# First sweep of a graph network: source rows gathered once per tile of edges into a ring, and copied from it slot by slot

## What is computed

```python
h = relu(layernorm(x))
# layer 0, GATv2, 4 heads of 64
m     = leaky_relu((h @ W_l + b_l)[src] + (h @ W_r + b_r)[dst] + edge_attr @ W_e)
alpha = einsum('ehf,hf->eh', m, att)          # a score per edge and head
a     = softmax of alpha over the edges of each dst (self loops too)
x     = x + relu(batchnorm(mean over heads of segment_sum((h @ W_l)[src] * a, dst) + bias))
# layer 1
h = relu(layernorm(x))
x = x + segment_mean(h[src], dst) @ w_l.T + h @ w_r.T + b
```

## Time and profile before

| what | us |
|---|---|
| median of 3 runs (5717.72 to 5723.28) | 5718.3 |
| the profiled execution | 5719.17 |
| its span, first to last instruction | 5717.8 |
| preparation, to the first transpose of the first sweep | 148.2 |
| first sweep, to VectorE's last copy | 148.2 to 2246.5 |
| maxima over segments | to about 2335 |
| second sweep | to about 3400 |
| third sweep | 3740 to 5660 |

### The profile page before, as it was taken

One profiled execution on the slowest core, in us unless ns is written; L12 is line 12 of the kernel. 1 busy time (PEld: TensorE's weight loads), 2 busy tenths in 40 slices (PEclk: granted clock), 3 DMA queues, 4 the chain that ended last, 5 costly groups with the idle time before them and its releaser, 6 DMA issues. The chain is left out here.

```text
span 5717.8 us, 78439 instructions
## 1 busy us (share of the span) xinstructions
PE 4023.6 (70%) x16956; PEld 2971.5 (52%) x16957; DVE 3389.3 (59%) x8725; ACT 1205.2 (21%) x4481; POOL 3734.5 (65%) x3702
## 2 busy tenths in 40 slices
PE   4888888888888886699999998454444444434445
PEld 3666666666666665344444456343333333333335
DVE  7666666666666666899999999732322322223223
ACT  2111111111111112566666645200000000000000
POOL 4677777777777775366556640167777777777774
PEclk9999999999999999799999998555555555555555
DMA  9444444444444443343434431211111111111112
GB/s 145 117 130 131 133 129 130 132 129 132 130 131 129 132 131 90 96 112 112 112 108 111 112 85 30 60 23 27 27 27 27 27 27 27 27 27 27 27 27 38
DMA packets 638020, 481.93 MB, mean 84 GB/s; under 512 B 453175, under 2 KB 464849, under 8 KB 637573
## 3 DMA queue, kind: packets, MB, share of 16 engines
q1 hardware_dynamic: 465852, 252.92, 17.5%
q0 software_dynamic: 104800, 108.55, 10.8%
q10 hardware_dynamic: 67177, 118.49, 5.7%
HBM read 351.85 MB, written 126.92 MB: 84 GB/s over the span
## 5 line engine op out<-in xcount | busy, mean ns | idle before, releaser
L586 POOL DMA_INDIRECT ZR<-hD,mS x1664 | 1589.0, 955 | 582.4 <-issue 492.6
L1361 POOL DMA_INDIRECT BIG<-h2D,mS x1564 | 1475.7, 944 | 706.7 <-issue 471.5
L1385 PE MATMUL PS<-BIG,ZR 128*128 x3328 | 805.1, 427 | 1128.3 <-SPq L1338 952.5
L1385 PEld LDWEIGHTS PS<-BIG,ZR 128*128 128x128 f32 x3328 | 737.3, 328 | 1196.1 <-SPq L1338 1016.7
L1404 DVE TENSOR_TENSOR BIG<-BIG,PS 128x64 f32 x1664 | 362.3, 218 | 1356.0 <-PE PS L1385 1319.7
L616 PE MATMUL PS<-Wz,R 128*128 128x264 f32 x3328 | 1062.6, 402 | 81.2 <-issue 80.3
L644 DVE SCALAR_TENSOR_TENSOR PS<-PS,a 128x528 f32<-128x528 f32 x832 | 596.0, 716 | 798.9 <-PE PS L617 792.1
L898 PE MATMUL PS<-R,ZR 128*128 128x329 f32 x3328 | 1025.9, 468 | 24.7 <-POOL R L884 16.9
L617 PE MATMUL PS<-BIG,R 128*128 x3328 | 1033.9, 393 | 0.0
L884 POOL TENSOR_TENSOR R<-ZR,R 128x768 f32<-128x768 f32 x416 | 615.8, 1480 | 414.2 <-ACT R L870 412.3
L912 DVE TENSOR_TENSOR BIG<-BIG,PS 128x329 f32 x1664 | 813.2, 489 | 13.4 <-PE PS L898 7.7
(11 more groups left out here) (258 smaller groups left out, 2319.6 us busy)
## 6 DMA issues: line engine op xcount, KB each, us to landing
zD<-ZR ACTq DMA_DIRECT2D x416, 256.0 KB, 2.2
ZR<-zD SPq DMA_DIRECT2D x416, 256.0 KB, 2.6
R<-relD SPq DMA_DIRECT2D x105, 512.0 KB
ZR<-ea SPq DMA_DIRECT2D x1664, 32.0 KB
ZR<-hD,mS POOLq DMA_INDIRECT x1664, 2.5
BIG<-h2D,mS POOLq DMA_INDIRECT x1564, 2.4
AL<-hD SPq DMA_DIRECT2D x28, 224.0 KB, 2.8
lmS<-lmD SPq DMA_DIRECT2D x106, 32.0 KB, 1.8
```

The lines of the kernel that those rows point to most:

```text
L586: Q.indirect_dma_start(zring[:, j % 32, 0, :], None, hD, bass.IndirectOffsetOnAxis(mS[:, j // 16, j % 16:j % 16 + 1], 0)).then_inc(hs[q], 16)
L1361: Q.indirect_dma_start(BIG[:, j * F:j * F + F], None, h2D, bass.IndirectOffsetOnAxis(mS[:, (j // 16) % 4, j % 16:j % 16 + 1], 0)).then_inc ...
L1385: ins = P.matmul(bank3(j // 4)[:, j % 4, :], oh[:, (j // 4) % 4, j % 4, :], rows, start=True, stop=True)
```

## The change

1. `gather_sources` makes one gather per tile (1564, written out without a loop), not per slot. Its target is a ring `HT` of 128 tiles, which lies over the end of `BIG` and the start of `R`. GpSimd itself waits for landings, two quads of gathers late, and counts them in `landed`. It may be 6 quads (24 tiles) ahead of the copies plus what the copies released (`hf`).
2. ScalarE's `keep_turned` copies each slot's rows (128 x 64) from the ring into `zring`, one quad ahead of TensorE. The ring's offset comes from registers (16 loaded from DRAM table `ringD` every 16 slots), and the number of landings to wait for from another 16 (table `needD`, every 64 slots). Its loop is now 64 slots long, not 32. TensorE waits for `hc` from ScalarE in place of the gathers' semaphores.
3. The source numbers come by one plain DMA (`dSr`) at the start. They are turned before the layer norm, and kept in SBUF: 256 columns in `lmS`, the others through `srcD` into the end of `AL`. The 13 indirect DMAs of source rows, `metaS` and SyncE's loads of it go away. `needD` is written twice.
4. `FLG` is loaded after the sweep, since the ring lies on its place: in two pieces by SyncE, of which VectorE awaits the second at the fourth of its 13 scans.

```diff
+    BR = sb("BR", [128, 26000 + NS * 4 + 16 * AC])
+    HT = BR[:, NB * MC:NB * MC + G * F]
...
+    dma(S, sI.rearrange("p (k e) -> p k e", e=128), src_t.rearrange("(k p) e -> p k e", p=128), dSr)
...
-        for o, t in ((dI, dst_t), (sI, src_t)):
-            dG.on(Q.indirect_dma_start(o[:, k, :], None, t,
-                                       bass.IndirectOffsetOnAxis(tI[:, 0, k:k + 1], 0)), 16)
+        dG.on(Q.indirect_dma_start(dI[:, k, :], None, dst_t, bass.IndirectOffsetOnAxis(tI[:, 0, k:k + 1], 0)), 16)
...
+    dSr.wait(A)
+    sa.on(A.copy(SF, sI))
+    sa.wait(P)
+    turned(SF, 4)
+    sp.wait(A)
+    kept(MS, 4)
+    sa.on(A.copy(first_src, MS[:, 0:256]))
+    sources_turned = sa.n
...
-        dma(S, needD[0, :].rearrange("(k p) -> p k", p=32), tN[3:128:4, :], dB)
+        dma(S, ringD[0, 12:12 + NS].rearrange("(k p) -> p k", p=128), tI3, dB)
+        for o in (0, NQ1 + 15):
+            dma(S, needD[0, o:o + NQ1].rearrange("(k p) -> p k", p=32), tN[3:128:4, :], dB)
+    S.wait_ge(sa.s, sources_turned)
+    dma(S, srcD, MS[:, 256:NG3], dM)
...
-    S.wait_ge(sa.s, sources_turned)
-    dma(S, metaS.rearrange("a p c -> p a c"), MS.rearrange("p (a c) -> p a c", c=16), dM)
...
-        dma(A, FLG, bass.AP(ff.tensor, 0, [[CH, 32], [0, 4], [1, CH + 1]]), dD)
...
+    dK.wait(Q)
+    Q.wait_ge(sa.s, sources_turned)
+    dma(A, more_src, srcD, dAI)
...
+    S.sem_inc(hf.s, 6)
...
-                if j % 16 == 4:
-                    msf.take(S)
-                    load_src(ds(i * 4 + half + 2, 1), (half + 2) % 4)
...
+        for t in range(NG3):
+            q = t // 4
+            if t == 256:
+                dAI.wait(Q)
+            if t % 4 == 0:
+                hf.take(Q)
+            at_src = first_src[:, t:t + 1] if t < 256 else more_src[:, t - 256:t - 255]
+            Q.indirect_dma_start(HT[:, (t % G) * F:(t % G) * F + F], None, hD, bass.IndirectOffsetOnAxis(at_src, 0)
+                                 ).then_inc(hs[q % 16], 16)
+            if t % 4 == 3 and q >= 2:
+                Q.wait_ge(hs[(q - 2) % 16], 64 * ((q - 2) // 16 + 1)).then_inc(landed, 1)
+        for q in (NG3 // 4 - 2, NG3 // 4 - 1):
+            Q.wait_ge(hs[q % 16], 64 * (q // 16 + 1)).then_inc(landed, 1)
...
                     if j % 4 == 0:
-                        P.wait_ge(hs[j // 4], 64)
+                        hc.take(P)
                         es[(j // 4) % 8].take(P, 64)
...
+        def source_row(reg, slot):
+            at_row = A.snap(reg, min_val=0, max_val=(G - 1) * F)
+            return A.copy(zring[:, slot % 32, 0, :], HT[:, ds(at_row, F)])
+
+        def some(i, last):
+            n = 15 if last else 16
+            A.load(needs[0:n], needD[0:1, ds(i * 16 + NQ1 + 16, n)])
+            for p in range(32):
+                q = p // 2
                 t_rdy.take(A)
+                A.copy(zo1[:, p % 2, :], PS[:, p % 2, 0:256]).then_inc(zo_rdy.s, 1)
+                if not (last and q == 15):
+                    if p % 8 == 0:
+                        n = 12 if last and q == 12 else 16
+                        A.load(offs[0:n], ringD[0:1, ds(i * 64 + 4 * q + 16, n)])
+                    if p % 2 == 0:
+                        gf.take(A)
+                        A.wait_ge(landed, A.snap(needs[q], min_val=1, max_val=NG3 // 4))
+                    for k in (2 * (p % 2), 2 * (p % 2) + 1):
+                        ins = source_row(offs[4 * (q % 4) + k], 4 * q + 4 + k)
+                        if k == 0:
+                            ins.then_inc(hf.s, 1)
+                        if k == 3:
+                            ins.then_inc(hc.s, 1)
...
+        A.load(offs[0:4], ringD[0:1, 12:16])
+        gf.take(A)
+        A.wait_ge(landed, 1)
+        for k in range(4):
+            ins = source_row(offs[k], k)
...
+        with A.Fori(0, NS // 64 - 1) as i:
+            some(i, False)
+        some(NS // 64 - 1, True)
...
+    cuts = (0, NS, CH + 1)
+    for k in range(2):
+        lo, hi = cuts[k:k + 2]
+        dma(S, FLG[:, lo:hi], bass.AP(ff.tensor, lo, [[CH, 32], [0, 4], [1, hi - lo]]), dD[k])
...
-    dD.wait(V)
-    V.wait_ge(stored, 1)
+    dD[0].wait(V)
...
+        if q == 3:
+            dD[1].wait(V)
```

More of the change, by code:

```diff
@@ L70, in build @@
     lmS = sb("lmS", [128, 4, 64])
+    first_src = lmS.rearrange("p a c -> p (a c)").bitcast(i32)
+    more_src = AL[:, 4 * NS - (NG3 - 256):4 * NS].bitcast(i32)
     sm = sb("sm", [128, 17, NB])
@@ L89, in build @@
     tabD = dram("tabD", [3, NS], i32)
[L90 removed]
+    NQ1 = NS // 4
+    needD = dram("needD", [1, 2 * NQ1 + 16], i32)
+    ringD = dram("ringD", [1, NS + 12], i32)
     flagD = dram("flagD", [1, NS * 128 + 1])
@@ L227, in build, with turned, kept @@
     sv.wait(Q)
-    dG, dB = dsem(), dsem()
     dI = tab(2).bitcast(i32).rearrange("p (k e) -> p k e", e=128)
-    sI = tab(3).bitcast(i32).rearrange("p (k e) -> p k e", e=128)
     for k in range(13):
-        for o, t in ((dI, dst_t), (sI, src_t)):
-            dG.on(Q.indirect_dma_start(o[:, k, :], None, t,
-                                       bass.IndirectOffsetOnAxis(tI[:, 0, k:k + 1], 0)), 16)
+        dG.on(Q.indirect_dma_start(dI[:, k, :], None, dst_t, bass.IndirectOffsetOnAxis(tI[:, 0, k:k + 1], 0)), 16)
+    SF, MS = tab(5), BIG[:, 29232:29232 + NS].bitcast(i32)
+    def turned(frm, bank):
+        for k in range(13):
+            sp.on(P.transpose(PS[:, bank + k // 4, (k % 4) * 128:(k % 4) * 128 + 128], frm[:, k * 128:k * 128 + 128], ident))
+    def kept(to, bank):
+        for q in range(4):
+            w = min(512, NS - 512 * q)
+            sa.on(A.copy(to[:, 512 * q:512 * q + w], PS[:, bank + q, 0:w]))
+        sa.wait(A)
+    dSr.wait(A)
[6 more added lines that the diff above has]
+    sources_turned = sa.n
     v(V.tensor_tensor(bst, sidx, cnt, ALU.subtract))
@@ L320, in build @@
     sv.wait(P)
-    RELf, SF, DFf, V1, V2 = tab(4), tab(5), tab(6), tab(7), tab(8)
+    RELf, DFf, V1, V2 = tab(4), tab(6), tab(7), tab(8)
     REL, DF = (t.rearrange("p (k e) -> p k e", e=128) for t in (RELf, DFf))
     RB = BIG[:, 31200:31200 + NS // 2].bitcast(bf16)
[L326 to L346, removed]
+    MR = BIG[:, 27536:27536 + NS + 32]
+    dG.wait(V)
     v(V.tensor_copy(DFf, tab(2).bitcast(i32)))
@@ L478, in build @@
     NQ = G // 4
[L479 to L486, removed]
+    hs, landed = sems("hs", 16), nc.alloc_semaphore("landed")
+    es, st, mr, mb, mf = flows("es", 8), flows("st", 8), flows("mr", 4), flows("mb", 2), flows("mf", 2)
+    gf, t_rdy, zo_rdy, oh_rdy, m_rdy, free1, wt_rdy, fin, hf, hc = flows("p1_", 10)
+    S.sem_inc(hf.s, 6)
     for q in st:
@@ L490, in build @@
     S.sem_inc(free1.s, 3)
[L491 to L496, removed]
     dM.wait(S)
-    for half in range(2):
-        load_src(ds(half, 1), half)
     def load_rel_turned(row, p):
@@ L572, in load_edges @@
                 S.dma_start(zring[:, j % 32, 1, :], ea[ds(et(j), 128), :]).then_inc(es[(j // 4) % 8].s, 16)
-            close(*st, *mf, msf)
+            close(*st, *mf)
     def gather_sources():
[L577 to L589, removed]
+        for t in range(NG3):
[11 more added lines that the diff above has]
+            Q.wait_ge(hs[q % 16], 64 * (q // 16 + 1)).then_inc(landed, 1)
+        close(hf)
     def score_products():
@@ L624, in score_products @@
                 products(p)
-            close(*es, oh_rdy, free1, zo_rdy)
+            close(*es, oh_rdy, free1, zo_rdy, hc)
     def keep_turned():
-        with A.Fori(0, NS // 32) as i:
-            for p in range(16):
-                t_rdy.take(A)
-                A.copy(zo[:, p % 2, :], PS[:, p % 2, 0:256]).then_inc(zo_rdy.s, 1)
-                if p % 2 == 1:
[L634 to L638, removed]
+        needs = [A.alloc_register(f"na{q}") for q in range(16)]
```

59 lines of the change are left out of this document (35 added, 24 removed).

## The result

The changed kernel takes 5585.0 us (median of 4 runs, 5581.4 to 5591.1), the kernel before 5718.0 (4 runs, 5717.2 to 5723.3): ratio 0.9766, 95% interval 0.975 to 0.9783. 5579.0 had been forecast, between 5556 and 5650. The profiled execution took 5581.35 us, its span is 5579.9; before 5719.17 and 5717.8.

What follows compares the result with a forecast made beforehand. GpSimd's gathers were taken to bound the first sweep. Fewer gathers 126.0 plus earlier start 27.2, minus tail 8.9 and `FLG` 4.9, gave 139.4 us less: span 5578.4, median 5579 us, range 5556 to 5650.

Steps and rivals of the forecast that it cites:

- What bounds the sweep: First sweep: GpSimd's gathers at 1.260 us each bound it, 80.6 us per 64 slots against TensorE's 70.3.
- Fewer gathers: First sweep: 1564 gathers instead of 1664, each at 1.260 us, save 126.0 us.
- the second pause: Start of first sweep: second quad freed behind two more register loads, about 146.6 us with GpSimd ready at 144.5; 2.1 lost.
- Waits on GpSimd: First sweep: GpSimd's added wait for landings and count per quad cost nothing visible, taken as 0.
- Rival 3: First sweep: waits on GpSimd show, costing 39 us, 5618 us in all; chance 0.07.
- An earlier start: Preparation and start of first sweep: three steps bring the freed gathers forward from 168.79 to 139.5 us; 27.2 us gained.
- Steps (b) and (c): Preparation: (b) ScalarE's cast and source copies leave the chain, 1.7 us; (c) its 64-byte table store goes, 3.4 us.
- The chain through ScalarE: First sweep: row copies and register loads stay hidden, about 71.3 us per 64 slots, under the gathers' 75.7.
- Rival 2: First sweep: five register loads stop TensorE in full, 86.8 us per 64 slots, 5868 us; chance 0.07 together with another rival.
- rival 1: First sweep: ScalarE and TensorE become the bound; at 78 us per 64 slots 5639 us; chance 0.19.
- The tail: End of first sweep: 21.5 us after the last gather instead of 12.6, because landings are counted two quads late; cost 8.9.
- `FLG`: Scans after first sweep: loading the flags only then holds them up, cost 4.9 us, between 0 and 9.

Runs made afterwards that it cites:

- g3: Changed kernel with a memset of 256 columns on GpSimd before each gather of the first sweep: 5880.4 us, ratio 1.0287 to the kernel before.
- g0: The changed kernel run again, unaltered: 5587.9 us, ratio 0.9772 to the kernel before.
- e11: Changed kernel with the 13 indirect loads of source rows put back into the preparation, into a tile nobody reads: 5586.3 us (one run).
- h1: Changed kernel with half the gathers left out after the 32nd quad and four row-offset loads per 64 slots doubled (only pointer loads were added): 5608.8 us.
- f9: Changed kernel with landings counted one quad late, six more quads at the start, and VectorE's comparison reading PSUM: 6907.2 us, ratio 0.9956 to the kernel before.
- f3: Changed kernel with ScalarE's load of landing counts per 64 slots doubled (only a pointer load was added): 6895.7 us, ratio 0.9944 to the kernel before.
- e1: Changed kernel with 97 more gathers in the first sweep, one after every 16th tile: 7035.4 us (one run).
- e2: Changed kernel with ScalarE's four row-offset loads per 64 slots doubled (only pointer loads were added): 7020.1 us (one run).
- e3: Changed kernel with the same edit as f3, in an earlier job: 6883.1 us, ratio 0.9919 to the kernel before.
- f1: Changed kernel with the same edit as e1, run once more: 7038.8 us, ratio 1.0153 to the kernel before.

## Why the prediction was right, point by point

*What bounds the sweep.* Confirmed by g3: 292.1 us computed from the pitch, 292.5 measured.

*Fewer gathers.* Taken at 1.260; measured (2081.35 - 136.13) / 1539 = 1.264, of which the second pause is 0.0014. So 4 us less gained than computed. The pitch differs from execution to execution (1.2640, 1.2679, 1.2649 in the changed kernel, g0 and e11), and 0.004 x 1539 = 6 us is most of what g0's profiled execution lies above that of the result (6.5 us).

*Waits on GpSimd.* Taken at 0. The wait for landings ended some 100 gaps, but none over 0.3 us. Rival 3 falls.

*An earlier start.* The last copy of the steps starts at 134.2 and ends at 134.5 (forecast 135.0), and e11 shows that VectorE's wait was worth 4.2 to 6.6 us there, in keeping with the 5.6 that I carried through. Steps (b) and (c) weren't tried alone; in all the first transpose comes 6.7 us earlier (forecast 7.3) and the last copy 11.2 (forecast 10.7). The 25th gather came at 136.13, not 139.5. The term that was mis-sized is the load ahead of the first row copies: I took 3.3 us, a load of 16 registers with its pointer. The first is of four registers and has no pointer:

```profile
L662 ACTq TENSOR_LOAD <-ringD x1: 757/757/757, 134.7 to 134.7; - x1
```

The second pause cost 2.45 - 0.30 = 2.1 us, as forecast.

*The chain through ScalarE.* 71.3 us per 64 slots forecast, 72.9 measured: the margin is 3.1 us rather than 4.4. The row copy was right (0.246 for 0.25), and the length of a load too; the rows of the changed kernel:

```profile
L646 ACTq TENSOR_LOAD <-ringD x104: 1778/2148/3405, 140.7 to 2077.6; - x104
...
L646 ACTq TENSOR_LOAD <-ringD_ptr x100: 1031/1102/2454, 139.5 to 2001.7; - x100
```

What was mis-sized is how much of the loads TensorE feels. I had put 1.0 us a pass beyond its own 70.3; it was 2.6. The starts of its transposes in the second to fifth pass (L603, means) say where. Across the three loads inside a pass it lost 0.3, 0.9 and 0.4 us beyond its own 0.86, where I took 0.1 to 0.3 each; why the middle one costs more is open. At the loop's end, where the fourth load of offsets and that of landing numbers stand, it lost 4.6 us, not 3.70. Rival 2 (3.3 us for every load) falls for the loads that the kernel has: most of their length is hidden. But the slack that hides them is used up by them, as h1 shows: there 1.0 us more on ScalarE was 1.0 us more of pass. So rival 1 was nearer than I had made it; four further pointer loads just bring the chain past the gathers' pace (76.9 against 76.0).

The Trainium skill's figure of about 200 ns per register (page Runtime: NRT & Kernel Launch, section Instruction fetch mechanics) would make 3.2 us of 16 registers; 2.15 were measured. Four took 757 ns, 189 each: the figure fits a short load and not a long one.

*The tail.* 2099.79 - 2081.35 = 18.4 us, forecast 21.5. *`FLG`.* Sweep's end to the tenth later scan's end: 2099.79 to 2125.20 = 25.4 us, and 2246.48 to 2267.67 = 21.2 before: 4.2 us for the 4.9 forecast, with the gap (2.15 us, 3 forecast) before the fourth scan.

*What had no term.* The last gather comes 152.5 us earlier; 5.8 are lost in the tail and 4.2 at the scans, which leaves 142.5, but the span is only 137.9 shorter. The rest, 4.6 us, goes in the second sweep, whose code is the same. VectorE's group in the changed kernel, with its idle time at the end:

```profile
L952 DVE TENSOR_TENSOR BR<-BR,PS 128x329 f32 x1664 | 814.0, 489 | 19.3 <-PE PS L938 11.7 <-issue 6.1
```

Before, the same group stood idle for 13.4 us; in g0, h1 and g3 it is 18.8 to 18.9. It is systematic, then, some 5.5 us on the engine that bounds that sweep, and from the group's first start to its last end the sweep takes 1038.3 us where it took 1034.2. In f9, whose edits leave that sweep's code alone too, the idle time is 14.9 us. Its cause is open: addresses and code positions moved with the change, and neither was tried alone.

In sum, against the forecast span of 5578.4: start 3.4 less, pitch 4.0 more, tail 3.1 and scans 0.7 less, second sweep 4.6 more, together 5579.8 where 5579.9 was measured. The forecast was near in part because these cancel. The rest of the 6 us is scatter: the median lies 3.6 us above the profiled execution, and I had put it 0.9 below.

## What to carry to other kernels

Where one engine's pitch fills a stage, price an edit by that pitch and prove it by drawing the instructions apart: a fixed pad on each should come back in full in the total. Where a chain is moved behind a busy engine, its slack is best read in the passes in which the old bound is ahead. A register load there costs the follower only what sticks out of the slack (0.3 to 0.9 us of 3.3 here); once the slack is used up, what is added is paid in full (1.0 of 1.0). Before an added instruction is priced, count it in the trace: a doubled load whose first result nobody reads was not there. Small gains at the start of a stage are read from start times, since the total's scatter hides them, but from several traces, for start times scatter as well (2.4 us here).

## What the runs showed that was not expected

On two of three chips the kernel before took 21% longer, and the first sweep's passes in f3 took 112 us instead of 76, with single waits of up to 8.7 us, but only while gathers ran: 72.5 us in f3 without them, 76.1 with half of them. The gathers themselves weren't slower (952 ns). The third sweep, which gathers too, took 2308 us from its first gather to its last in f3 against 1976 in the changed kernel; the second, without gathers, 1037.9 against 1038.3. What the change gains on such chips is known only for f3, with a pointer load more per pass: 0.6%, not 2.3%. Why those chips behave so isn't settled; the run that was to test it by drawing gathers apart came to an undisturbed chip.

In f9, where a two-operand comparison with an operand in PSUM replaces VectorE's one-operand comparison of SBUF data, the gather's mean is 943 ns, the third sweep's figure; in e1, e2, e3, f1 and f3 it is 949 to 953. VectorE's instruction went from 0.49 to 0.68 us. The Trainium skill (page SBUF — State Buffer, section SBUF: two separate sides) says that a VectorE operation in a two-port mode keeps GpSimd from writing descriptors. The 6 to 10 ns per gather agree with it in direction; that this lock is their cause wasn't shown, since only the whole instruction was exchanged, and f9 held two other edits.
